# Expert layer of six out of 16: every expert on every token, replaced by a dispatch of token rows in two halves

## What is computed

```
p   = softmax(h @ gate_w.T)                  # [T, 16]
w,e = top_k(p, 6);  w = w / sum(w)           # six experts a token, with weights
out = sum_k w[:, k] * ((silu(h @ eg_w[e_k].T) * (h @ eu_w[e_k].T)) @ ed_w[e_k].T)
    + (silu(h @ sg_w.T) * (h @ su_w.T)) @ sd_w.T        # shared part, every token
x   = x + out
```

## Time and profile before

| | |
|---|---|
| profiled execution: its time | 4948.9 us |
| its span (first to last instruction) | 4947.2 us |
| median of the timed runs | 4942.24 us |
| TensorE busy | 4205.8 us, 85% of the span |
| VectorE, ScalarE, GpSimd busy | 2622.0, 2039.2, 887.2 us |
| mean granted TensorE clock | 0.915 of full speed |
| HBM traffic | 93.03 MB read, 22.94 MB written |

### The profile page before, as it was taken

How to read it: one execution, slowest core, us unless ns; L and a number is a source line. 1 busy time by engine, 2 the same in 40 slices (tenths; PEclk the granted TensorE clock), 3 DMA queues, 4 the chain that set the end, 5 groups by cost and what they waited for, 6 DMA issues and landing times. The chain is left out here.

```text
span 4947.2 us, 74700 instructions
## 1 busy us (share of the span) xinstructions
PE 4205.8 (85%) x25323; PEld 3379.0 (68%) x25324; DVE 2622.0 (53%) x5961; ACT 2039.2 (41%) x5254; POOL 887.2 (18%) x714
## 2 busy tenths in 40 slices
PE   5886999999786874799999999699989998888692
PEld 3554899999564753678777778577767776565671
DVE  5787988987454334444443444433333333676633
ACT  4775666665122431333333333333333332666140
POOL 1002333332000420000000000122222222000145
PEclk9897999999897985899999999899999999899596
DMA  1001000000001001200000000100010000000344
GB/s 60 16 13 41 1 0 0 0 0 1 30 15 39 1 24 47 69 5 5 5 1 5 5 5 5 62 5 9 9 50 10 9 9 18 14 11 7 95 134 127
DMA packets 100239, 119.04 MB, mean 24 GB/s; under 512 B 13776, under 2 KB 81200, under 8 KB 99760
## 3 DMA queue, kind: packets, MB, share of 16 engines
q1 hardware_dynamic: 93152, 97.25, 6.1%
q0 software_dynamic: 6864, 18.75, 1.4%
HBM read 93.03 MB, written 22.94 MB: 23 GB/s over the span
## 5 line engine op out<-in xcount | busy, mean ns | idle before, releaser
L1145 ACT ACTIVATE peer_tab<-peer_sims 128x128 f32<-128x128 f32 x1024 | 305.6, 392 | 0.0
L1152 POOL TENSOR_TENSOR peer_tab<-peer_sims 128x2048 f32<-128x2048 f32 x64 | 244.6, 3842 | 290.0 <-ACT peer_sims L1129 260.8
L1200 DVE SCALAR_TENSOR_TENSOR peer_tab<-peer_tab,peer_th 128x2048 f32<-128x2048 f32 x128 | 294.9, 2346 | 0.3
L1624 DVE COPY mha_ks<-bank 128x512 f32<-128x512 f32 x128 | 88.5, 691 | 353.3 <-PE bank L1589 350.8
L1217 PE MATMUL bank<-ident,peer_tab 128*128 128x128 f32 x2048 | 247.0, 274 | 20.0 <-DVE peer_tab L1200 20.0
L1217 PEld LDWEIGHTS bank<-ident,peer_tab 128*128 128x128 f32 x2048 | 233.7, 142 | 33.6 <-DVE peer_tab L1200 21.2
L1267 PE MATMUL bank<-peer_wd,peer_hh 128*128 128x256 f32 x1024 | 242.1, 380 | 1.8 <-DVE peer_hh L1258 1.8
L1729 PE MATMUL bank<-mha_wo,mha_oT 128*128 128x256 f32 x1024 | 242.1, 379 | 0.0
L1240 PE MATMUL bank<-peer_hT,peer_wg 128*128 128x256 f32 x1024 | 241.9, 379 | 0.0
L643 DVE TENSOR_TENSOR moe2a_b<-moe2a_a,bank 128x512 f32<-128x512 f32 x104 | 71.6, 688 | 296.4 <-PE bank L556 273.2
L631 POOL TENSOR_TENSOR moe2a_hh_lo<-moe2a_hh,moe2a_hh_hi 128x512 fp32r<-128x512 f32 x104 | 141.1, 1356 | 401.4 <-ACT moe2a_hh_hi L622 385.5
(11 more groups left out here) (519 smaller groups left out, 11143.1 us busy)
## 6 DMA issues: line engine op xcount, KB each, us to landing
m_y_rows<-moe_y SPq DMA_DIRECT2D x79, 128.0 KB
att_ctxT<-in_ctxT_dram SPq DMA_DIRECT2D x32, 256.0 KB, 2.6
x<-in_x_dram SPq DMA_DIRECT2D x4, 1024.0 KB, 9.4
lin_ctxT<-in_ctxT_dram SPq DMA_DIRECT2D x16, 256.0 KB, 2.7
mem_ctxT<-in_ctxT_dram SPq DMA_DIRECT2D x16, 256.0 KB, 2.8
mem_ctx<-in_ctx_dram SPq DMA_DIRECT2D x16, 256.0 KB, 2.9
t_scratch<-mha_hTf SPq DMA_DIRECT2D x8, 512.0 KB, 2.7
moe2a_hTf<-t_scratch SPq DMA_DIRECT2D x8, 512.0 KB, 3.6
```

Source lines behind the costliest of these rows:

```text
L1145: i = nc.scalar.activation(tab[g][h][:, b * P:(b + 1) * P], sims[:, g, h, P:2 * P], ACT.Identity, bias=sims[:, g, h, b:b + 1])
L1152: nc.gpsimd.tensor_tensor(out=tab[g][h][:].rearrange("p (a b) -> p a b", b=P), in0=sims[:, g, h, P:2 * P].unsqueeze(1).broadcast_to([P, NB ...
L1200: nc.vector.scalar_tensor_tensor(out=tab[g][h][:], in0=tab[g][h][:], scalar=th[:, g, h:h + 1], in1=tab[g][h][:], op0=ALU.is_ge, op1=ALU.mu ...
L1624: nc.vector.tensor_copy(ks[:, s % 2, :], K[:]).then_inc(ks_ready, 1)
```

## The change

The two calls of `ffn_stage` are replaced by one new stage, `routed_shared_stage`. It is a dispatch like the last stage, with these differences:

- 2048 tokens are a half. For each half, 96 indirect DMAs from GpSimd (16 groups x 6) write token rows to their places in a DRAM tensor (scatter); SyncE fetches blocks of 128 rows from it with plain DMAs. A half has 2048 x 6 / 128 + 15 = 111 blocks of a fixed count, both 222.
- The shared part is done as 64 "static items" (32 groups x 2 parts of 176 columns) with plain fp32 operands: 40 of them before the 222 blocks, 24 after.
- Gate and up products of a block are six matmuls 352 columns wide in fp32r (two halves of D times three split parts). The high and low parts of all expert weights are made at the start of the stage, those of the rows in each block. The down product is two plain fp32 matmuls (128 and 48 hidden columns).
- 192 indirect DMAs bring results back: 96 beside the second half's blocks, 96 after the last block.
- In the attention stage before, `tail_sp` also stores the rows untransposed, and 14 DMAs write zeros to all places of both halves (29.1 MB).

The routing (`route_dve`, `weights_dve`, `count_pe`, `base_dve`, `slots_dve`) is that of the last stage with six choices instead of two: six VectorE operations over 512 columns for each choice, a multiplication and a sum over 512 columns for each choice's places, and no token lists. After it VectorE finds the expert of each block (`experts_dve`, two comparisons of 1776 columns) and makes the low parts of the weights (`split_dve`, four operations of 2816 columns), and only then starts its loop over the items.

The core of the diff:

```diff
+BLOCKS_HALF = T // 2 * 6 // P + 15
...
+        if some(t - 1):
+            dve.wait_ge(rows_stored, 16 * (t - 1))
...
     def tail_sp(sp, t):
+        sp.wait_ge(tn_ready, t + 1)
+        sp.dma_start(core.h_rows.rearrange("(g p) d -> p g d", p=P)[:, bass.ds(t * GT, GT), :], x1[:]).then_inc(rows_stored, 16)
         sp.wait_ge(t_emptied, (t + 1) * C)
...
+            sp.wait_ge(zero_set, 1)
+            for h in range(2):
+                places = core.places[h].rearrange("(b p) d -> p b d", p=P)
+                for b in range(0, BLOCKS_HALF, 16):
+                    n = min(16, BLOCKS_HALF - b)
+                    sp.dma_start(places[:, b:b + n, :], zero[:].unsqueeze(1).broadcast_to([P, n, D])).then_inc(places_zeroed, 16)
             tail_sp(sp, 0)
...
+    E, K, I, NSH = 16, 6, 176, 2
+    HG = NG // 2
+    GT, NT = 2, NG // 2
+    NBH = BLOCKS_HALF
+    NBLK = 2 * NBH
+    NIN, NY, NR = 6, 4, 8
+    NS1 = 40
+    NS = NG * NSH
+    ITEMS = NS + NBLK
...
+    def load_tile_sp(sp, u):
+        t = u % NT
+        if NT > u >= 2:
+            sp.wait_ge(logits_ready, u - 1)
+        if NT + 2 > u >= NT:
+            sp.wait_ge(logits_ready, u - 1)
+        if u >= NT + 2:
+            sp.wait_ge(gu_ready, share_end(t - 2))
...
+    def scatter_pool(pool, g, k):
+        t = g // GT
+        if g % GT == 0 and k == 0:
+            pool.wait_ge(src_in[t % 2], 16 * (t // 2 + 1))
+        nc.gpsimd.indirect_dma_start(out=core.places[g // HG], out_offset=bass.IndirectOffsetOnAxis(ap=slot_u[:, k, g:g + 1], axis=0),
+                                     in_=src[t % 2][:, g % GT, :], in_offset=None).then_inc(scattered[t % 2], 16)
+
+    def fetch_sp(sp, b):
+        if b % NBH == 0:
+            for i in range(2):
+                sp.wait_ge(scattered[i], 16 * GT * K * (b // NBH + 1) * NT // 4)
...
+    def block_rest_dve(dve, b):
+        dve.wait_ge(hTh_ready, b + 1)
+        nc.vector.tensor_tensor(out=hTl[b % 2][:].rearrange("p c t -> p (c t)"), in0=TB[b % 2][:, 0:D],
+                                in1=hTh[b % 2][:].rearrange("p c t -> p (c t)"), op=ALU.subtract).then_inc(hT_ready, 1)
...
+    def gate_up_pe(pe, i, e):
+        if i >= 2:
+            pe.wait_ge(hh_ready, i - 1)
+        if static(i):
+            g, n = share(i)
+            t = g // GT
+            pe.wait_ge(hTf_in[t % 2], 16 * ((NT + t) // 2 + 1))
+            pairs = [(hTf[t % 2][:, c, (g % GT) * P:(g % GT + 1) * P], wgu[:, c, n, :, :].rearrange("p k i -> p (k i)")) for c in range(C)]
+        else:
+            b = block(i)
+            pe.wait_ge(hT_ready, b + 1)
+            if b == 0:
+                pe.wait_ge(wlo_made, 4)
+            pairs = [(left[b % 2][:, c, :], right[:, c, bass.ds(e, 1), :, :].rearrange("p e k i -> p (e k i)"))
+                     for c in range(C) for left, right in ((hTh, whi), (hTl, whi), (hTh, wlo))]
+        for n, (left, right) in enumerate(pairs):
+            j = nc.tensor.matmul(GB[i % 2][:, 0:2 * I], left, right, start=(n == 0), stop=(n == len(pairs) - 1))
+        j.then_inc(gu_ready, 1)
...
+        nc.scalar.activation(hhT[i % 2][:, 0, :], HB[i % 2][:, 0:P], ACT.Copy)
+        nc.scalar.activation(hhT[i % 2][0:I1, 1, :], HB[i % 2][0:I1, P:2 * P], ACT.Copy).then_inc(hhT_ready, 1)
...
+        if n >= NR:
+            pool.wait_ge(added, n - NR + 1)
...
+            for i in range(-1, ITEMS + 2):
+                if NS1 - 1 <= i < NS1 + NBLK - 1:
+                    block_turn_pe(pe, block(i + 1))
+                if 0 <= i < ITEMS:
+                    who_of[i] = None
+                    if not static(i):
+                        if block(i) == 0:
+                            pe.wait_ge(ids, 8)
+                        who_of[i] = pe.value_load(who_i[0:1, block(i):block(i) + 1], min_val=0, max_val=E - 1)
+                    gate_up_pe(pe, i, who_of[i])
+                if 0 <= i - 2:
+                    down_pe(pe, i - 2, who_of[i - 2])
+                if 0 <= i - 1 < ITEMS:
+                    hidden_turn_pe(pe, i - 1)
...
+            for i in range(-1, ITEMS + 2):
+                if 0 <= i - 1 < ITEMS:
+                    silu_act(act, i - 1)
+                if NS1 - 1 <= i < NS1 + NBLK - 1:
+                    block_turned_act(act, block(i + 1))
+                if 0 <= i - 2:
+                    hidden_turned_act(act, i - 2)
...
+            dve.wait_ge(gate_in, 32)
+            for n in range(4):
+                split_dve(dve, n)
+            n = 0
+            for i in range(0, ITEMS + 3):
+                if 0 <= i - 1 < ITEMS:
+                    hidden_dve(dve, i - 1)
+                if NS1 <= i + 1 < NS1 + NBLK:
+                    block_rest_dve(dve, block(i + 1))
+                if 0 <= i - 3:
+                    result_dve(dve, i - 3)
+                if n < HG * K and i >= item(NBH) + 12:
+                    add_dve(dve, n)
+                    n += 1
+            assert n == HG * K
+            for n in range(HG * K, NG * K):
+                add_dve(dve, n)
...
+            pool.wait_ge(slot_ready, 1)
+            for g in range(NG):
+                for k in range(K):
+                    scatter_pool(pool, g, k)
+            for h in range(2):
+                stored_pool(pool, h)
+                for n in range(h * HG * K, (h + 1) * HG * K):
+                    return_pool(pool, n)
...
-            ffn_stage(core, "moe2a", "gated", "scratch", blocks=13, top_k=6)
-            ffn_stage(core, "moe2b", "gated", "scratch", blocks=12, top_k=6, first=13)
+            routed_shared_stage(core)
```

More of the change, by code:

```diff
@@ L61, in __init__ @@
         self.neghalf = ctx.enter_context(nc.sbuf_tensor("neghalf", [P, 16], FP32))
+        self.h_rows = nc.dram_tensor("h_rows", (T, D), FP32, kind="Internal").ap()
+        self.places = [nc.dram_tensor(f"places{h}", (BLOCKS_HALF * P, D), FP32, kind="Internal").ap() for h in range(2)]
+        self.results = [nc.dram_tensor(f"results{h}", (BLOCKS_HALF * P, D), FP32, kind="Internal").ap() for h in range(2)]
         self.x_in = ctx.enter_context(nc.semaphore("x_in"))
@@ L1441, in self_attention_stage @@
     tT = hTf
+    zero = sb("zero", [P, D])
+    zero_set, places_zeroed, rows_stored = sem("zero_set"), sem("places_zeroed"), sem("rows_stored")
     Q, K, V, Y = bank[0], bank[1], bank[2], bank[6:8]
@@ L1738, in tail_dve @@
         dve.wait_ge(f_filled, (t + 2) * C if not (isinstance(t, int) and t == NT - 1) else NT * C)
+        if isinstance(t, int) and t == NT - 1:
+            dve.wait_ge(rows_stored, 16 * t)
         for g in range(GT):
@@ L1866, in _ @@
             sp.wait_ge(stored, 16 * NT)
+            sp.wait_ge(rows_stored, 16 * NT)
+            sp.wait_ge(places_zeroed, 16 * 2 * -(-BLOCKS_HALF // 16))
         @block.tensor
@@ L1910, in _ @@
             nc.gpsimd.memset(pT[:], 0.0).then_inc(zeroed, 1)
+            nc.gpsimd.memset(zero[:], 0.0).then_inc(zero_set, 1)
             front_pool(pool, 0)
```

398 lines of the change are left out of this document (added).

## The result

The changed kernel takes 5094.5 us (median of 4 runs) beside 4944.8 for the kernel before on the same chip: a ratio of 1.030, 95% interval 1.028 to 1.032. Forecast were 4853 us, with 0.10 for slower. The profiled execution took 5094.2 us.

The account below looks back on a forecast made before the run. TensorE's own work was taken to bound the expert layer (998 of 1041 us). First block at 212, blocks to 795, static tail to 853, returns to 966, next stage at 969 instead of 1057.6: 4942 - 89 = 4853 us, 8-in-10 range 4795 to 4935.

Parts of the forecast that it names:

- First scatter possible: Start of the new stage: logits to 38, routing 27 and places 15 more, with weights loaded meanwhile; T = 84.
- Scatter of the first half: After the places: 96 indirect DMAs at 1.25 us each, priced like the last stage's returns, 120 us, ending at T = 204.
- First block: After scatter, last landing 2.7, first fetch 2.5, turning and splitting 2: first block at T = 212.
- The cover of the first 90 us of scatter: Before the blocks: 40 static items at 2.3 us on TensorE hide behind the scatter, ending at T = 201.
- Blocks: Middle of the stage: 222 blocks at 2.63 us, 583 us, the second half's scatter beside the first half; ending at T = 795.
- The price of a block: TensorE per block: gate and up 1.06, down 0.86, hidden turns 0.22, row turn 0.11, gap 0.38; 2.63 us.
- The gap of 0.38: Between second row turn and next block's first product, where the expert number is loaded into a register; kept in the price.
- the rival's mechanism: Faster blocks: register load and gap hide behind longer products, 2.36 us a block, -60, 4793 us; chance 0.13.
- Static tail and returns: After the blocks: 24 items at 2.3, 55 us, 3 to drain, 88 returns at 1.25, 110 us, and 3.3; T = 966.
- the one for slower: Rival: a scatter costs 2.5 us, +120, 4973 us; the sign turns above 2.2 us a DMA; chance 0.09.
- The lock: Rival: VectorE operations with two SBUF inputs lock out GpSimd, holding up scatter and first block 17 us: 4870 us; chance 0.12.
- Hand-over bound blocks: Rival: the down product waits for ScalarE copies, blocks take 3.0 us instead of 2.63, +82, 4935 us; chance 0.13.

Follow-up runs that it names:

- the kernel with plain stores: Changed kernel with each scatter replaced by a plain GpSimd DMA of the same bytes to consecutive places (output not the reference's): 4914.4 us, 0.994 of before.
- equal rows: Changed kernel with the down product's second part padded by zeros from 48 to 128 rows: 4982.6 us.
- the last gather kernel: Changed kernel with gathers by token list instead of scatters, 128 rows everywhere, lists in their own bank, 24 static items ahead of the blocks: 4812.4 us, 0.972 of before.
- two other kernels: Equal rows, two scatters in flight and returns beside the last static items: 4858.8 us; and the last gather kernel: 4812.4 us.

## Why the prediction was wrong

The step that failed is the overlap: the prediction let the scatter lie beside TensorE's work at no cost, before the blocks and beside the first half's. The runs show 180 us in its place. By its terms, from the stage's first DMA: the forecast put the next stage at 969, it came at 1206.8, 238 us later.

- **First scatter possible**, forecast 84: 86.9. Logits, routing and places hold. (For the places the sum takes off 3 us for two operations that take 2.5, from 4653.64 to 4656.15.)
- **Scatter of the first half**, 1.25 us each: 1.26 in a burst. The price that I had asked about was right. What I didn't ask is what a scatter does to the others. The prediction's own test for an error in structure, TensorE idle for more than 20 us before the first block beside a running scatter, came true, with 60 us in nine gaps. But it was badly set: the forecast's own plan has TensorE idle from 84 to 106, and even the kernel with plain stores is idle for 26 us there.
- **First block**, forecast 212: 311.5 on TensorE, +99.5. With plain stores it comes at 210.3. (The prediction's own terms, 204 + 2.7 + 2.5 + 2, make 211.2.) The cover of the first 90 us of scatter, 40 static items at 2.3, became 5.2 each: the scatter slowed what should have hidden it. Undisturbed they take 2.59.
- **Blocks**, forecast 583: 699.4, +116. Of this (2.783 - 2.63) x 222 = 34 is the price of a block (two errors that half cancel, next item), (3.479 - 2.783) x 110 = 77 the second half's scatter beside the first half, 5 in the second half. I had listed that scatter as lying beside the blocks at no cost.
- **The price of a block** was right in its sum of products and wrong in two places that half cancel. The gap of 0.38 that I kept is gone (the rival's mechanism), and 0.34 us for the two changes between 128 and 48 rows was missing (0.09 and 0.20 in the two parts of the down product, 0.05 at the hidden turns). The rows I went by could not show it, since all their products have 128 rows. The Trainium skill ("TensorEngine Tiling (Array Packing)", section "Key Properties") says that a change of the tiling mode, and not only of the tile, drains TensorE; if a product of 48 rows runs in another mode than one of 128, which no run here shows, the longer distances are drains by that rule, and the trace agrees with it as far as it goes (0.62 and 0.63 against 0.53 and 0.43 with equal rows). I had not weighed it.
- **Static tail and returns**, forecast 171: 181, +10; items 2.6 instead of 2.3, with the same loss at the 48 rows, and 88 returns 1.25 apart as forecast (the last line of the windows above, TensorE idle).
- **To the next stage**, forecast 2.6: 14.7, +12. After the last addition (4323.5 to 4324.0) nothing is recorded until the next weights at 4338.7. In the last gather kernel the same stretch is 10.6. What fills it was not tried.
- **Attention and zeroing** at nothing: 1.0 us, within the spread of the runs.

99.5 + 116 + 10 + 12 = 238. Of it 101 + 77 = 178 goes with the indirect form of the scatter (plain stores: 180), 34 with the price of a block (the rows cost 76, the vanished gap gave back the rest). Without the scatter's effect the change would have gained 30 us (0.994), not 89.

The rivals: the one for slower had the right part and the wrong mechanism; 2.5 us a scatter was not met, and its point of decision (2.2 us) says nothing here. **The lock** is seen: while VectorE made the low parts of the weights from 3227.6 on, four scatters took 2.76 us instead of 0.96. Timeline of the changed kernel:

```profile
3227.57 12.33 DVE L3580 SCALAR_TENSOR_TENSOR moe_wlo<-moe_wlo,moe_ln,moe_whi 128x2816 fp32r<-128x2816 f32 x4
3228.79 2.76 POOL L3531 DMA_INDIRECT places<-moe_src,moe_slot_u  x1 [0.30 <-issue]
3231.85 2.76 POOL L3531 DMA_INDIRECT places<-moe_src,moe_slot_u  x1 [0.30 <-issue]
```

With two more of 2.72 and 1.60 before them that is 9.6 us of GpSimd's time, half of the 17 by the Trainium skill's rule ("SBUF — State Buffer", section "SBUF: two separate sides"), which the prediction took the returns to speak against. Here the trace agrees with it. Hand-over bound blocks: not seen, the undisturbed pace is 2.78 for another reason.

Open: why indirect DMAs delay TensorE's updates. For the 180 us it takes the indirect form (plain DMAs of the same bytes cost nothing), the direction to DRAM (gathers in the same places cost no completion) and no pauses between them; that much is shown. Not shown are whether the pauses help by the lower rate or by the fewer scatters under way at once, why the returns of two other kernels delay updates too, and the path on which the updates wait.

## What to carry to other kernels

An operation that no row shows has two prices: its own time, and what it does to the engines beside it. Bound both, and test the second by replacing it with a plain form of the same bytes. Where GpSimd must write rows to scattered places beside TensorE's work, leave it pauses or gather on the reading side, and look at the consumers of TensorE's results either way. At 2.3 us between starts no completion is late, but the scatter itself takes longer and may then be what all wait for, as in the front here (5015.5 us, where at most two in flight gave 4973.6). Try one number of rows in all products of a loop, with zeros if need be: here it brought 0.34 us of 2.78.

## What the runs showed of the hardware

- Indirect writes from GpSimd at 1.26 us a piece delay TensorE's semaphore updates by up to 12 us; at 2.3 us a piece they don't, with 160 GB/s and a DMA share of 0.51 in the window. Plain stores 0.53 us apart in a burst and gathers 1.25 apart in the scatters' places delayed none. Returns (indirect reads) 1.25 apart beside static items delayed five of 23 copies, by up to 4.9 us; a gather and a return in each block of the gather kernel 42 of 89, by 1.2 us.
- A product of 48 rows between products of 128 costs TensorE 0.34 us a block beside the same product with 128 rows: 0.09 where it follows them, 0.25 behind it.
- In 13 runs the granted clock of the whole kernel went from 0.882 to 0.905; the four with over 90 us of late completions had the lowest, 0.882 to 0.884, as the changed kernel has. In its stretches with gaps the clock is 0.66 to 0.86 on average, between its levels of 1.2 and 2.4 GHz. So a late completion was paid twice, in waiting and in slower products behind it.
